# A GRU and two mixtures of experts on one core: weight loads in half-megabyte parts, recurrent weights in natural order, and a shorter set-up

## The chip, the cores and the metric

The kernel runs as one program on one core of a Trainium2 chip. The metric is the device time of one execution in microseconds (us), lower is better. It is written in Bass: each engine has its own instruction list, and every dependency between engines is a semaphore that the kernel sets and waits for by hand.

## The reference, cut to what matters

x is [4, 512, 512] (batch, time, features), D = 512. Three things are computed one after another:

```python
def cell(h, x):                       # scan over 512 time steps
    gi = x @ W_ih + b_ih              # does not depend on h
    gh = h @ W_hh + b_hh
    r = sigmoid(i_r + h_r); z = sigmoid(i_z + h_z)
    n = tanh(i_n + r * h_n)
    h_new = (1 - z) * n + z * h
x = x + ffn0(hs)     # x @ W.T + a mixture of 8 LoRA experts of rank 16, top 2
x = x + ffn1(interp(x, grid))   # linear interpolation along features, then per token
    # the top 2 of 8 experts: h = x @ w1[e].T + b1[e] (1024 columns), y = glu(h), y @ w2[e].T + b2[e]
```

All inputs are float32. The kernel splits an operand into a high and a low float16 part (scaled by 16 for activations, 64 for weights) and takes three products (high by high, low weight by high, high weight by low) in place of one float32 product.

## The kernel before, in words

**Order of the work.** The recurrence is a chain of 512 steps that cannot be shortened by other work, so everything else is hung between its steps by hand. The 512 steps fall into 4 groups of FT = 128. A step `gru(t)` is, on PE, 16 matmuls with the low recurrent weights on an early high part of h (L611), 16 with the high weights on both parts of h (L617), both for the gates r and z, then 4 bias matmuls (L623) and 32 for the gate n (L629). Each writes 32 PSUM partitions, so four run side by side. DVE then transposes (L1281, L1285), sums (L1283), scans (L1287, L1293) and splits the new h; ACT makes the sigmoid and the tanh (L978, the line of the helper `run`). POOL copies h to a history tile (`keep`, L1664).

**Group 0 (steps 0 to 127)** carries the prelude. The input gates `gi` of 64 time steps are one visit: 144 matmuls of 256 columns (L639, `gi_piece`). Visit 0 is made before step 0, visits 1 to 7 are spread over the steps in slots (`FIRST = 16` steps a visit to step 63, `LATER = 21` after it). The expert weights (16 halves of 1536 KB) are loaded, split by ACT and DVE, and stored to HBM; tables such as `MOE_STORE`, `MOE_LOAD`, `X_LOAD`, `GI_STORE` and `ZERO` name the step at which SP issues each transfer.

**Groups 1 to 3** run steps 128 to 511, and between them the feed-forward part of the block of 128 time steps that the group before has finished. After a head of 29 steps come NT = 15 tiles of 128 picked tokens, one expert each, 6 steps (u = 0 to 5) a tile (`slot`): u 0 to 2 the 26 up matmuls (24 of 128x512, L840, and two bias matmuls L836 with 2 rows), u 3 and 4 the 12 down matmuls (L860), u 3 and 5 transposes (L822, L846) and parts of the neighbours. A tail of 9 steps gathers the results and adds them.

**The last block** runs without any recurrence, its 15 tiles back to back. It has 4 weight buffers where the groups have 2: the tiles of `whh` and `gi` are free by then.

**Weights.** A tile needs 3072 KB: `load_up` (L494) issues 1536 KB (L500), 512 KB (L501) and 4 KB of biases (L502) one behind the other, and `load_down` (L504) 1024 KB (L509). For the tiles from the ninth on, the expert's number is read from a tile into a register of SP first (`value_load`, L491). SP issues all this in the order of its own list; what paces it are the waits for `up_mm`, `down_mm`, `d_out` and `xt_mm`. The input gates come back in one transfer of 1536 KB (L523).

**Recurrent weights.** They lie in `whh` in an order of their own: for each of the 4 strips of 32 columns the three gates one behind the other, so that the moving operand of a matmul is one run of 256 or 128 columns (L612, L630). The split at the start writes that order (`strips`): 12 activations of 128x512 and 48 DVE operations of 128x128 (L1646).

**The start.** SP loads the first third of `W_ih`, then x, six small arrays, the other two thirds, three constants and the three thirds of `W_hh` (L397 to L407), 1024 KB each third. PE waits for `x_split` and `wih_split`, makes visit 0, then a bias row through two matmuls of its own (L947), and waits for `whh_split` 3 before step 0 (L950). ACT makes `gates_now(0, 0)` (L1252) once all of this is out.

Of the kernel before, what the change touches and what calls it, by code (L numbers as in the profile page):

```python
# [24 lines left out]
UPW = K * 2 * D  # L25
PER = 5
# [37 lines left out]
def loads(f, j):  # L64

    if f < FB - 1:
# [5 lines left out]
VISITS = (0, 7, 6, 5, 1, 4, 3, 2)  # L72
KEPT = (0, 4, 7)
FIRST, LATER = 16, 21
# [29 lines left out]
X_LO = [s + q for s in (13, 21, 35, 56, 67, 91) for q in range(2)]  # L104
# [3 lines left out]
           for j, s in enumerate(at)}  # L108
# [11 lines left out]
X_LOAD = {2: 2, 16: 3, 30: 4, 38: 5, 59: 6, 69: 7}  # L120
L0_LOAD = {3: 0, 17: 1, 35: 2, 57: 3}
GRID_LOAD = {7: 1, 39: 2, 66: 3}
GI_STORE = {14: (1, 0), 19: (1, 1), 28: (2, 0), 32: (2, 1), 41: (3, 0), 49: (3, 1), 78: (5, 0), 86: (5, 1), 96: (6, 0),
            115: (6, 1)}
ZERO = {s: j for j, s in enumerate((5, 8, 11, 15, 18, 20, 21, 22, 25, 29, 31, 42, 45, 48, 51))}
ROW_STORE = {B2_AT + 3: 0, B1_AT + 5: 1}
PUT = {s for table in (MOE_STORE, MOE_LOAD, X_LOAD, L0_LOAD, GRID_LOAD, GI_STORE, ZERO, ROW_STORE) for s in table}
# [8 lines left out]
GIS = {v: pieces(G3, len(GI), n) for v, n in [(1, FIRST - 2)] + [(v, FIRST if v < 5 else LATER) for v in range(2, NB)]}  # L136
GIS[1] = [[], []] + GIS[1]

# [6 lines left out]
def visit(s):  # L145

    v, at, n = (1 + s // FIRST, s % FIRST, FIRST) if s < TB else (5 + (s - TB) // LATER, (s - TB) % LATER, LATER)
    return (v, at, n) if v < NB else (None, 0, 0)
# [12 lines left out]
def adaln_ffn_kernel(nc, x, h0, grid, w_ih, w_hh, b_ih, b_hh, w_base, lora_a, lora_b, w_router,  # L161
# [7 lines left out]
    with ctx:  # L169
# [41 lines left out]
        bias_w = sb("bias_w", [P, K], F32)  # L211
        bias_s = sb("bias_s", [P, 2, K], F16)
# [58 lines left out]
        b1s = upto[:, 0:E].rearrange("p e (g k) -> p e g k", g=2)  # L271
        spare_rows = hxs[:, FB % 2].rearrange("p a k b t -> p (a k b t)")
# [17 lines left out]
        bias_d = x1_f[:, 3 * D:4 * D].bitcast(F16).rearrange("p (w k n) -> p w k n", w=2, k=K)  # L290
        bias_at = gm[:, 1, 0, 0, 0:2 * P].rearrange("p (w n) -> p w n", w=2)
# [7 lines left out]
        def unit(i, n=1):  # L299
# [46 lines left out]
            const_in bias_in b2_in mix_zero l0_in x_in grid_in block_in row_stored zeroed  # L346
# [48 lines left out]
        def _(sp):  # L395
# [155 lines left out]
            for f in range(FB - 1):  # L551
# [4 lines left out]
                if f:  # L556
                    store_out(f - 1)
# [1248 lines left out]
```

## Time and profile before

| | |
|---|---|
| median of the 3 runs | 1904.66 us |
| all runs | 1902.78, 1904.66, 4286.78 us |
| the profiled execution's own time | 1901.47 us |
| its span in the trace | 1899.6 us |
| granted TensorE clock, mean | 0.999 |
| busy: PE, DVE, ACT, POOL | 91%, 69%, 41%, 16% |
| step 0 starts on PE | 36.01 us |
| steps 0 to 511 | 36 to 1699 us |
| last block | 1699 to 1899.6 us |

Times in the views are microseconds from the start of the span. PE is the matmul part of TensorE, PEld its weight loads, DVE VectorE, ACT ScalarE, POOL GpSimd, SP the engine that issues the transfers. "L611" is line 611 of the kernel. A busy PE is not PE at its peak: matmuls are pipelined, and one of 128x512 that is shown with 0.38 us starts some 0.22 us after its neighbour. An idle time ahead of an instruction is followed by what ended it; "issue" means that the engine waited for nothing that the profile shows.

### The profile page before, as it was taken

The numbers are of one execution on the slowest core, as the hardware profiler recorded it, in microseconds if no ns is written. First come the engines' busy times: TensorE is split into PE (matmuls) and PEld (weight loads), VectorE is DVE, ScalarE is ACT, GpSimd is POOL, SyncE is SP. The second block draws the span as 40 slices with busy tenths as digits, with TensorE's granted clock in tenths as the row PEclk, the third lists the DMA queues.
The fourth block names the chain that finished last, engine by engine and source line by source line (L and its number), as shares of the span: only waits on it lengthen the run. The fifth ranks groups of instructions, "written<-read, shape, count | busy, mean of one in ns | idle before, by whom it ended". The sixth has DMA issues, their size and how long they took to land.

```text
span 1899.6 us, 94495 instructions
## 1 busy us (share of the span) xinstructions
PE 1728.6 (91%) x40920; PEld 1153.3 (61%) x40920; DVE 1302.3 (69%) x5832; ACT 777.1 (41%) x2709; POOL 299.8 (16%) x601
## 2 busy tenths in 40 slices
PE   5888888878889999998999999988999999988998
PEld 4666676666556566656666566655666566654444
DVE  6788887877767676777766667777777666764323
ACT  5555566643334343332333343432334334323343
POOL 2222222221211111121211001121211001121001
PEclk9999999999999999999999999999999999999999
DMA  6445334345225465426134565426136445339993
GB/s 246 148 165 197 134 147 187 154 176 191 97 88 214 173 227 200 158 76 220 64 129 162 192 232 183 161 66 206 59 138 224 162 176 215 111 96 371 404 372 112
DMA packets 112945, 333.97 MB, mean 176 GB/s; under 512 B 41848, under 2 KB 42000, under 8 KB 100112
## 3 DMA queue, kind: packets, MB, share of 16 engines
q1 hardware_dynamic: 107408, 311.15, 45.0%
q0 software_dynamic: 5120, 16.78, 2.7%
q8 instruction: 320, 5.24, 1.1%
q14 instruction: 97, 0.79, 0.1%
HBM read 263.09 MB, written 64.78 MB: 173 GB/s over the span
## 4 chain that ended last, share of the span: by engine, by line
PE 70%; DVE 16%; ACT 6%; issue 5%; DMA 2%; DVEq 0%; SPq 0%; POOL 0%; ACTq 0%
PE bank L840 17%; PE bank_g L611 15%; PE bank_g L617 12%; PE bank L860 8%; PE bank_g L629 7%; DVE xt L1281 5%; DVE na L1287 3%; DVE pre L1283 3%; ACT rz L978 3%; DVE hs_early L1293 3%; ACT seq_h L978 3%; PE bank L654 2%; PE bank L836 2%; PE bank_l L846 2%; PE bank L822 2%
## 5 line engine op out<-in xcount | busy, mean ns | idle before, releaser
L1664 POOL COPY hxs<-hs 128x32 f16<-128x32 f16 x512 | 225.7, 441 | 1385.8 <-DVE hs L1301 1385.6
L978 ACT ACTIVATE rz<-pre 128x32 f32<-128x32 f32 x512 | 125.7, 245 | 750.9 <-DVE pre L1283 750.1
L611 PE MATMUL bank_g<-whh,hs_early 128*32 128x256 f16 x8192 | 319.0, 275 | 113.2 <-DVE hs_early L1293 110.3
L1281 DVE STREAM_TRANSPOSE xt<-bank_g 128x256 f32<-128x256 f32 x512 | 230.6, 450 | 226.6 <-PE bank_g L617 216.3
L611 PEld LDWEIGHTS bank_g<-whh,hs_early 128*32 128x32 f16 x8192 | 172.0, 96 | 298.7 <-DVE hs_early L1293 287.4
L629 PE MATMUL bank_g<-whh,hs 128*32 128x128 f16 x16384 | 323.3, 219 | 14.6 <-issue 14.4
L617 PE MATMUL bank_g<-whh,hs 128*32 128x256 f16 x8192 | 315.0, 273 | 4.3 <-issue 4.1
L840 PE MATMUL bank<-wm,wih 128*128 128x512 f16 x1272 | 308.6, 381 | 5.2 <-issue 3.0
L629 PEld LDWEIGHTS bank_g<-whh,hs 128*32 128x32 f16 x16384 | 257.4, 97 | 19.4 <-issue 18.5
L617 PEld LDWEIGHTS bank_g<-whh,hs 128*32 128x32 f16 x8192 | 206.4, 96 | 25.8 <-issue 5.7
L978 ACT ACTIVATE seq_h<-na 128x16 f32<-128x16 f32 x512 | 115.1, 225 | 215.9 <-DVE na L1287 215.9
L1293 DVE TENSOR_TENSOR_SCAN hs_early<-omz,seq_h 128x32 f16<-128x32 f32 x512 | 119.7, 234 | 104.9 <-ACT seq_h L978 104.7
L840 PEld LDWEIGHTS bank<-wm,wih 128*128 128x128 f16 x1272 | 110.0, 98 | 131.1 <-issue 15.2
L978 ACT ACTIVATE wih<-bank 128x512 f32<-128x512 f32 (+2 forms) x208 | 145.0, 701 | 90.5 <-PE bank L822 39.4
L1287 DVE TENSOR_TENSOR_SCAN na<-rz,xt_n 128x48 f32<-128x48 f32 x512 | 132.0, 258 | 72.9 <-ACT rz L978 3.9
L1285 DVE STREAM_TRANSPOSE xt_n<-bank_g 128x128 f32<-128x128 f32 x512 | 162.6, 318 | 14.6 <-PE bank_g L629 14.3
L639 PE MATMUL bank<-hxs,wih 128*128 128x256 f16 x1152 | 151.1, 278 | 16.1 <-DVE hxs L1306 13.0
L860 PE MATMUL bank<-wm,wih 128*128 128x512 f16 x636 | 154.0, 380 | 1.4 <-issue 1.4
L1283 DVE TENSOR_REDUCE pre<-xt 128x32 f32<-128x96 f32 x512 | 129.6, 253 | 17.6
L639 PEld LDWEIGHTS bank<-hxs,wih 128*128 128x128 f16 x1152 | 103.6, 99 | 41.7 <-DVE hxs L1306 13.0
L978 ACT ACTIVATE xt<-gi 128x32 f32<-128x32 f32 x512 | 123.7, 242 | 0.0
L1301 DVE TENSOR_TENSOR hs<-hh,hs_early 128x16 f16<-128x16 f32 x512 | 119.9, 234 | 0.0
(237 smaller groups left out, 2062.3 us busy)
## 6 DMA issues: line engine op xcount, KB each, us to landing
wm<-moe_split SPq DMA_DIRECT2D x53, 1536.0 KB
wm<-moe_split SPq DMA_DIRECT2D x53, 1024.0 KB, 6.4
wm<-moe_split SPq DMA_DIRECT2D x53, 512.0 KB
wm<-in_w_moe SPq DMA_DIRECT2D x16, 1536.0 KB, 6.8
moe_split<-wm SPq DMA_DIRECT2D x16, 1536.0 KB, 5.7
wih<-x_rows SPq DMA_DIRECT2D x58, 256.0 KB, 7.8
y_rows<-wih SPq DMA_DIRECT2D x58, 256.0 KB, 4.2
xr<-in_x SPq DMA_DIRECT2D x16, 512.0 KB, 6.7
```

Of the source, the lines that this page charges most:

```text
L611: mm(bank_g[0][32 * j:32 * j + 32, 0:2 * P], early_cols[:, 8 * B * k:8 * B * (k + 1)], whh[:, 1, k, at:at + 2 * P], start=(k == 0), stop=F ...
L617: i = mm(bank_g[0][32 * j:32 * j + 32, 0:2 * P], hs_cols[:, 8 * B * k:8 * B * (k + 1)], whh[:, 0, k, at:at + 2 * P], start=False, stop=(k ...
L629: i = mm(bank_g[1][32 * j:32 * j + 32, 0:P], hs_cols[:, 8 * B * k:8 * B * (k + 1)], whh[:, w, k, at:at + P], start=False, stop=(k == K - 1 ...
L639: i = mm(bank[m % len(bank)][:, 0:N], wih[:, w, k, m * P:(m + 1) * P], xs[v % 2][:, a, k], start=(j == 0), stop=(j == len(GI) - 1))
L840: mm(bk[:, :], xgt[:, a, k], weights(f, j)[:, at // HALF, w, up_at(at)], start=(c == 0), stop=False)
L860: i = mm(bank_down[:, :], yt[:, a, k], weights(f, j)[:, 1, w, up_at(UPW + k * D)], start=(n == 0), stop=(n == len(DOWN) - 1))
L978: return nc.scalar.activation(dst, src, func, **kw)
L1281: link(V.transpose(rows, bank_g[0][:, 0:2 * P].rearrange("p (m c) -> p m c", c=32)))
L1283: V.tensor_reduce(pre[:, :, :], terms, AX, ALU.add).then_inc(S["rz_pre"], 1)
L1287: V.tensor_tensor_scan(pairs["na"], pairs["r"], pairs["seq_n"], 0.0, ALU.mult, ALU.add).then_inc(S["n_pre"], 1)
L1293: V.tensor_tensor_scan(early_scan, pairs["omz"], pairs["seq_h"], 0.0, ALU.mult, ALU.add).then_inc(S["h_hi"], 1)
L1664: Q.tensor_copy(hxs[:, par, :, :, :, col].rearrange("p s k b -> p s (k b)"), hs_new).then_inc(S["h_kept"], 1)
```

## The change

- The start is reordered. x comes first, then `W_ih` in four parts (512, 512, 1024 and 1024 KB), h, the recurrent bias twice as a row, `W_hh` in three parts, and the small arrays and constants last. POOL makes the sum of the gate biases.
- Only the first 32 of the 64 time steps of the first visit are made ahead (visit 0, 144 matmuls of 128 columns); the other 32 are visit 1, in steps 0 to 7, 18 matmuls a step. The next four visits have 14 steps each (`WINDOW`) where they had 16.
- `whh` keeps its natural order. Its split is 3 activations and 3 DVE operations of 128x2048; the moving operand of a recurrent matmul is now 8 runs of 32 columns (r and z) or 4 runs (n and the bias), a run every 128 columns (`strip`).
- The bias row is built on POOL, ACT and DVE, without matmuls.
- A tile's weights come in 6 parts of 512 KB (`load_up` 4, `load_down` 2), each [128, 2, 1024] float16. In groups 1 to 3 SP waits for `h_ready` ahead of every step's transfers and issues one part a step (`load_head`, `load_slot`); the blocks of x and out and the gates come in parts of 512 KB too. In the prelude, the halves of 1536 KB are loaded and stored in two parts, in steps that follow each other. In the last block the parts are issued without such waits. `expert_of` is called for each part.
- The bias matmuls of the up product have 128 rows where they had 2; the other 126 rows are cleared once, by POOL, at step 120 and in group 3 behind step 19.
- Some steps of the tables move by a few.

```diff
-VISITS = (0, 7, 6, 5, 1, 4, 3, 2)
-KEPT = (0, 4, 7)
-FIRST, LATER = 16, 21
+VISITS = (0, 0, 7, 6, 5, 1, 4, 3, 2)
+WINDOW = {1: (0, 8), 2: (8, 14), 3: (22, 14), 4: (36, 14), 5: (50, 14), 6: (64, 21), 7: (85, 21), 8: (106, 21)}
...
-MOE_LOAD = {s + (3 if n < 13 else 2): n + 2 for s, n in MOE_STORE.items() if n + 2 < 2 * E}
+MOE_LOAD = {s + (2 if n in (6, 10, 11, 12, 13) else 3): n + 2 for s, n in MOE_STORE.items() if n + 2 < 2 * E}
+MOE_PUT = {s + part for table in (MOE_STORE, MOE_LOAD) for s in table for part in range(2)}
...
-        def strips(w, q, k):
-
-            by_strip = whh[:, w, k].rearrange("p (j g m c) -> p g m j c", j=K, g=3, c=32)
-            return by_strip[:, q]
+        def strip(v, j):
+
+            return v.rearrange("p (g j c) -> p j g c", j=K, c=32)[:, j]
...
         def _(sp):
+            sp.dma_start(xv, x[0]).then_inc(S["x_in"], 16)
+            for c in range(2):
+                sp.dma_start(wih_part(wm32[0], c), wih_part(w_ih, c)).then_inc(wih_in[c], 16)
+            for dst, src in ((bi[:, :], b_ih), (bh[:, :], b_hh)):
+                sp.dma_start(dst, src).then_inc(S["gate_bias_in"], 16)
+            for c in range(2, 4):
+                sp.dma_start(wih_part(wm32[0], c), wih_part(w_ih, c)).then_inc(wih_in[c], 16)
+            sp.dma_start(h_in, h0.rearrange("p k b -> p (k b)")).then_inc(S["h0_in"], 16)
+            sp.wait_ge(S["bias_zero"], 1)
+            for row in range(2):
+                sp.dma_start(bias_f[32 * row:32 * row + 1, :].rearrange("o (m p) -> o m p", m=K),
+                             b_hh[:, 2 * K:].rearrange("p (o m) -> o m p", o=1),
+                             allow_slow_non_contiguous=True).then_inc(S["bias_row_in"], 16)
             for q in range(3):
...
+            def load_half(n, part):
+                lo, hi = part * HALF // 2, (part + 1) * HALF // 2
+                sp.dma_start(wm32[0][:, n % 2 * HALF + lo:n % 2 * HALF + hi], w_moe[n, :, lo:hi]
+                             ).then_inc(stage_in[n % 2], 16)
...
+            def load_up(f, j, n):
+                if n == 0 and (f or j > 1):
                     sp.wait_ge(S["up_mm"], 2 * (f * NT + max(j + 1 - ring(f), 0)))
                 e = expert_of(f, j)
...
+                sp.dma_start(place_of(f, j, n), piece_of(e, n)).then_inc(up_in[j % ring(f)], 16)
+                if n == K - 1:
+                    if j in (0, 2):
+                        sp.wait_ge(S["rows_zero"], 1 if j % ring(f) < 2 else 2)
+                    sp.dma_start(ring_b[j % ring(f)][0:2], up_bias[e]).then_inc(up_in[j % ring(f)], 16)
...
+            def load_slot(f, j, u):
+
+                g = f + 1
+                if u == 0 and 1 <= j < NT - 1:
+                    load_up(f, j + 1, K - 1)
+                if u == 0 and j in (7, 9, 11) and g + 1 < FB:
+                    gi_load(2 * g + 2, 0, (j - 7) // 2)
+                if u in (1, 2) and j >= 2:
+                    load_down(f, j, u - 1)
+                if u == 1 and j >= 2:
+                    store_y(f, j - 2)
+                if u == 2 and j + 2 < NT:
+                    load_rows(f, j + 2)
+                if u >= 3 and j + 2 < NT:
+                    load_up(f, j + 2, u - 3)
...
             for f in range(FB - 1):
...
+                for s in range(20):
+                    sp.wait_ge(S["h_ready"], (f + 1) * FT + s + 1)
+                    load_head(f, s)
                 for j in range(NT):
...
+                    for u in range(SLOT):
+                        sp.wait_ge(S["h_ready"], (f + 1) * FT + HEAD + j * SLOT + u + 1)
+                        load_slot(f, j, u)
...
                     for j in range(K):
-                        at = j * 3 * P
-                        mm(bank_g[0][32 * j:32 * j + 32, 0:2 * P], early_cols[:, 8 * B * k:8 * B * (k + 1)],
-                           whh[:, 1, k, at:at + 2 * P], start=(k == 0), stop=False)
+                        mm(out_strip(0, j, 2 * P), early_cols[:, 8 * B * k:8 * B * (k + 1)],
+                           strip(whh[:, 1, k, 0:2 * D], j), start=(k == 0), stop=False)
...
                     if k is None:
-                        mm(bk[:, :], ones_as[0:2, :], ring_b[j % ring(f)][0:2, half * D:(half + 1) * D],
+                        mm(bk[:, :], ones_as[:, :], ring_b[j % ring(f)][:, half * D:(half + 1) * D],
                            start=False, stop=True).then_inc(S["up_mm"], 1)
...
+            x_hi(0)
+            wih_hi(0)
+            wih_hi(1)
+            wih_hi(2)
+            act.wait_ge(S["bi_ready"], 1)
+            gi_out(0, 0)
+            gi_out(0, 1)
+            wih_hi(3)
...
+            whh_hi(2)
+            for m in range(9, G3):
+                gi_out(0, m)
+            x_hi(2)
             act.wait_ge(S["gi_done"], G3)
             gates_now(0, 0)
...
-            for q in range(3):
-                for k in range(K):
-                    dve.wait_ge(S["whh_hi"], q * K + k + 1)
-                    for m in range(K):
-                        i = stt_(strips(1, q, k)[:, m], part_of(wm32[1], q)[:, k, m * P:(m + 1) * P].rearrange(
-                            "p (j c) -> p j c", c=32), WS, strips(0, q, k)[:, m], ALU.mult, ALU.subtract)
-                i.then_inc(S["whh_split"], 1)
+            whh_lo(0)
+            dve.wait_ge(S["bias_hi"], 1)
+            low = slice(32, 32 + 1)
+            stt_(bias_n[low], bias_f[low], WS, bias_n[low], ALU.mult, ALU.subtract).then_inc(S["bias_row"], 1)
+            whh_lo(1)
+            whh_lo(2)
             for s in range(FT):
...
+                if f == FB - 2:
+                    pool.wait_ge(S["l0_mm"], (f + 1) * K)
+                    Q.memset(spare_rows[:, 0:4 * D], 0.0).then_inc(S["rows_zero"], 1)
```

Here `wih_part` is `part_of` with the first gate cut in two, `out_strip` names the same PSUM region as before, `x_of(v)` is the number of the x load that visit v uses, and `piece_of` and `place_of` are part n of an expert's weights in HBM and in the buffer. `load_head` does for the first 20 steps of a group what `load_slot` does for the tiles: the block's x in steps 0 and 1, the last block's out in steps 2 and 3, the 12 parts of tiles 0 and 1 in steps 4 to 15, the gates in 16 to 18, the wait for `scattered` and the first rows in 19.

## Rows read from the trace of the kernel before

**Rows 1.** The profile's page: the chain that ended last, by engine

```profile
PE 70%; DVE 16%; ACT 6%; issue 5%; DMA 2%; DVEq 0%; SPq 0%; POOL 0%; ACTq 0%
```

**Rows 2.** Windows: length, busy PE, PEld, DVE, ACT, POOL, clock, DMA share, GB/s

```profile
447.00:865.00 418.00, 394.69 (x9838) 256.86 (x9836) 294.89 (x1400) 153.59 (x608) 60.57 (x144) 1.00 0.45 159
...
1780.00:1820.00 40.00, 40.00 (x232) 18.34 (x231) 13.51 (x21) 14.62 (x21) 0.00 (x0) 1.00 1.01 388
```

**Rows 3.** Timeline, steps 1 and 2: start, length, engine, line, tiles, count

```profile
42.27 0.62 PE L611 MATMUL bank_g<-whh,hs_early 128*32 128x256 f16 x16 [1.57 <-DVE hs_early L1293]
...
43.77 1.27 PE L639 MATMUL bank<-hxs,wih 128*128 128x256 f16 x10
...
45.41 0.62 PE L611 MATMUL bank_g<-whh,hs_early 128*32 128x256 f16 x16 [0.38 <-DVE hs_early L1293]
...
45.85 0.61 PE L617 MATMUL bank_g<-whh,hs 128*32 128x256 f16 x16
```

**Rows 4.** Waits of PE (total us, times, longest): issue, first and last of seven

```profile
PE bank_g L629 <- issue: 14.4, 21, 1.6
...
PE bank_g L623 <- issue: 1.0, 1, 1.0
```

**Rows 5.** Timeline of PE around one such wait

```profile
636.83 0.56 PE L629 MATMUL bank_g<-whh,hs 128*32 128x128 f16 x28
638.72 0.24 PE L629 MATMUL bank_g<-whh,hs 128*32 128x128 f16 x4 [1.33 <-issue]
```

**Rows 6.** Window ahead of it, columns as in rows 2

```profile
630.50:636.00 5.50, 5.50 (x132) 3.35 (x128) 4.46 (x21) 2.22 (x10) 0.33 (x1) 1.00 0.94 336
```

**Rows 7.** Timeline of SP's issues ahead of it

```profile
626.87 0.55 SPq L501 DMA_DIRECT2D wm<-moe_split  x1
...
632.73 0.55 SPq L509 DMA_DIRECT2D wm<-moe_split  x1
```

**Rows 8.** The profile's page: the queue of PE's instructions (packets, MB, share)

```profile
q8 instruction: 320, 5.24, 1.1%
```

**Rows 9.** Timeline of PE, slots u = 1 and 2 of a tile

```profile
604.24 0.62 PE L611 MATMUL bank_g<-whh,hs_early 128*32 128x256 f16 x16
...
605.73 1.47 PE L840 MATMUL bank<-wm,wih 128*128 128x512 f16 x6
607.13 0.39 PE L836 MATMUL bank<-brow,ones_as 2*128 2x512 f16 x1
607.44 0.62 PE L611 MATMUL bank_g<-whh,hs_early 128*32 128x256 f16 x16
```

**Rows 10.** Timeline of PE, last block, one tile to the next

```profile
1749.33 0.39 PE L836 MATMUL bank<-brow,ones_as 2*128 2x512 f16 x1
...
1758.85 0.39 PE L836 MATMUL bank<-hxs,ones_as 2*128 2x512 f16 x1
```

**Rows 11.** Timeline of the start

```profile
14.13 1.91 ACT L978 ACTIVATE wih<-wm 128x2048 f16<-128x2048 f32 x1 [5.03 <-DMA wm<-in_w_ih]
...
16.07 2.29 DVE L1623 SCALAR_TENSOR_TENSOR wih<-wm,wih 128x2048 f16<-128x2048 f32 x1 [3.17 <-ACT wih L978]
...
22.12 2.95 DVE L1635 TENSOR_SCALAR upto<-upto 128x32 f32<-128x32 f32 x1
...
26.17 9.79 DVE L1646 SCALAR_TENSOR_TENSOR whh<-wm,whh 128x128 f16<-128x128 f32 x48
...
36.01 0.62 PE L611 MATMUL bank_g<-whh,hs_early 128*32 128x256 f16 x16 [0.65 <-DVE whh L1646]
...
36.99 0.62 PE L629 MATMUL bank_g<-whh,hs 128*32 128x128 f16 x32
...
38.86 0.23 DVE L1293 TENSOR_TENSOR_SCAN hs_early<-omz,seq_h 128x32 f16<-128x32 f32 x1 [0.21 <-ACT seq_h L978]
```

**Rows 12.** Window over the first 21 us, columns as in rows 2

```profile
0.00:21.00 21.00, 6.76 (x48) 5.29 (x48) 8.32 (x7) 9.15 (x8) 3.89 (x14) 1.00 0.90 299
```

**Rows 13.** SP's register loads in the last block: ns min/median/max

```profile
L491 SPq TENSOR_LOAD <-eid x14: 273/430/445, 1781.3 to 1851.9; - x14
```

More of the change, by code:

```diff
@@ L25 @@
 UPW = K * 2 * D
+WIDTH = 1024
 PER = 5
@@ L103 @@
 GRID_HAT = {s + 3 + 4 * k: (b, k) for b, s in enumerate(GRID_START) for k in range(K)}
-X_LO = [s + q for s in (13, 21, 35, 56, 67, 91) for q in range(2)]
+X_LO = [s + q for s in (13, 31, 40, 56, 67, 91) for q in range(2)]
 L0_AT = (10, 24, 44, 65)
@@ L133, in pieces @@
     return [flat[s * len(flat) // slots:(s + 1) * len(flat) // slots] for s in range(slots)]
-GIS = {v: pieces(G3, len(GI), n) for v, n in [(1, FIRST - 2)] + [(v, FIRST if v < 5 else LATER) for v in range(2, NB)]}
-GIS[1] = [[], []] + GIS[1]
+GIS = {v: pieces(G3, len(GI), n) for v, (first, n) in WINDOW.items()}
 def ended(v, at):
@@ L145, in visit, with x_of @@
 def visit(s):
-    v, at, n = (1 + s // FIRST, s % FIRST, FIRST) if s < TB else (5 + (s - TB) // LATER, (s - TB) % LATER, LATER)
-    return (v, at, n) if v < NB else (None, 0, 0)
+    for v, (first, n) in WINDOW.items():
+        if first <= s < first + n:
+            return v, s - first, n
+    return None, 0, 0
+def x_of(v):
+    return max(v - 1, 0)
 def before(h, par):
@@ L366, in adaln_ffn_kernel @@
         gathered = [sem(f"gathered_{b}") for b in range(B)]
-        wih_in = [sem(f"wih_in_{gate}") for gate in "rzn"]
+        wih_in = [sem(f"wih_in_{part}") for part in ("r_a", "r_b", "z", "n")]
         whh_in = [sem(f"whh_in_{gate}") for gate in "rzn"]
@@ L438, in _ @@
             sp.dma_start(g_in, grid[0:1].to_broadcast([P, D])).then_inc(S["grid_in"], 16)
-            sp.wait_ge(S["wih_split"], 3)
-            load_half(0)
-            load_half(1)
+            sp.wait_ge(S["wih_split"], 4)
+            for n in range(2):
+                for part in range(2):
+                    load_half(n, part)
             sp.wait_ge(S["zero_set"], 1)
@@ L579, in _ @@
             sp.wait_ge(S["h_ready"], FB * FT + 1)
-            load_block(f)
-            store_out(f - 1)
+            for q in range(2):
+                load_block(f, q)
+            for q in range(2):
+                store_out(f - 1, q)
             for j in range(LAST_RING):
-                load_up(f, j)
-                load_down(f, j)
+                for n in range(K):
+                    load_up(f, j, n)
+                for n in range(2):
+                    load_down(f, j, n)
             sp.wait_ge(S["scattered"], FB * B * 2 * 16)
@@ L1358, in prelude @@
                 if s in (0, 1):
-                    x_lo(1, s)
+                    x_lo(2, s)
+                if s == 0:
+                    dve.wait_ge(S["bias_in"], 16 * 3)
+                    step(ts_(b1s[:, :, 1], b1s[:, :, 1], 1.0, None, ALU.add))
+                    step(ts_(bg[:, :], bg[:, :], PS, None, ALU.mult))
                 if s == B2_AT + 1:
@@ L1634, in _ @@
             step(V.memset(rz[:, 0:K * B, 1:GROUP - 1], 1.0))
-            step(ts_(b1s[:, :, 1], b1s[:, :, 1], 1.0, None, ALU.add))
-            step(ts_(bg[:, :], bg[:, :], PS, None, ALU.mult))
+            step(V.memset(ws_col[:, :], WS))
+            x_lo(0, 0)
+            x_lo(0, 1)
+            for c in range(4):
+                wih_lo(c)
+            dve.wait_ge(S["h0_in"], 16)
             step(ts_(hh[:, :, 1:2], h_in.unsqueeze(2), AS, None, ALU.mult))
```

324 lines of the change are left out of this document (156 added, 168 removed).

## The prediction

> **What bounds the kernel now.** I read the chain that ended last first [rows 1]: 70% of it is PE, 16% DVE, 6% ACT, and 5% is "issue", time in which an engine had work and nothing to wait for. By stage [rows 2], a group of 128 steps takes 418 us with the transfers at a share of 0.45, while the last block runs with them at 1.01. A step of the recurrence is fixed by its own chain: L611 starts at 42.27 and again at 45.41, 3.14 us later, and with ten matmuls of a visit in it PE still waits 0.38 us for h [rows 3]. 512 such steps are 1607 us. From 36 to 1699 us are 1663, so the steps lose some 56 us in all. Half of that can be named: in the view of waits PE stands at "issue" in seven groups of 36 waits, from 14.4 us (21 waits, up to 1.6) down to 1.0, which sum to 27.7 us [rows 4].
>
> One of them close up [rows 5]: L629 is cut after 28 of its 32 matmuls at 636.83, and the last 4 come at 638.72, with 1.33 us of nothing between. The transfer engines were at 0.94 in the 5.5 us before [rows 6], because SP had issued the 1536 KB of L500 and behind them the 512 KB of L501 at 626.87, and 1024 KB more at 632.73 [rows 7]. PE's own instructions come over the same 16 engines: 320 packets, 5.24 MB, so 16 KB a packet [rows 8], one every 5.9 us. My reading: a packet that is asked for while one large transfer fills the engines comes when that transfer is through, 3 to 4 us late, and PE's store of instructions covers less than that.
>
> **Parts of 512 KB, one a step.** At the 388 GB/s of a full queue [rows 2] 512 KB take 1.4 us, and with rows or y (256 KB) in the same step 2.1 us. Then the engines are free until the next step, 3.14 us after the last. A packet waits 2 us at most where it waited 4. The bytes stay the same: 3584 KB a tile over six steps is 195 GB/s, half of what the queue gives. Bounds: nothing gained, and all 27.7 us. I take 23: a few will be left in the prelude, where a part is 768 KB (2.1 us) and can meet a gate store of 768 KB or an x load, and where a gate part and a weight part fall in one step. SP has 1.3 us of work for a part with a register load (0.43 for the load [rows 13], 0.3 for the checks behind it, 0.55 for the transfer [rows 7]), of 3.14. The last up part goes out at u = 0 and is needed at u = 5, the down parts eight steps ahead of their use; 15 and 25 us are many times what the data take. The new waits on `h_ready` stand in SP's list only, and behind them are only the transfers of later steps; `store_y` and `load_rows` move by at most two steps within buffers that are two tiles deep. Nothing for them.
>
> The Trainium skill speaks against both halves of this. Its page "Runtime: NRT & Kernel Launch", section Instruction fetch mechanics, says that blocks of 16 KB are fetched ahead and that crossing a block is mostly hidden; by it the waits at issue have another cause and the sum loses its 23 us. The block size agrees with the trace; the rest I don't take, since the gap stands behind a stretch of full engines [rows 5, 6]. Its page "DMA: Bandwidth & Descriptors", section Bandwidth, advises transfers of 1 MiB and more for three quarters of the peak. In the groups half the peak is enough; in the last block it would matter (a rival below).
>
> **The bias matmuls of 128 rows.** In a row of 128x512 matmuls one starts every 0.217 us (six in 1.47, of which the last shows 0.385) [rows 9]. The sixth of these starts at 606.81 and L836 at 607.13, 0.31 later; L611 follows after 0.31 again. The next step's start is 3.20 us after the last where rows 3 have 3.14. So a change to 2 rows and back costs PE 0.1 us each way. With 128 rows the matmul itself costs the same, for its 512 columns set its time. In the groups two steps of a tile are long by 0.06 to 0.08: 90 x 0.07 = 6.3 us. In the last block PE alone sets the pace: a tile follows the last after 9.52 us [rows 10], with three such intervals in it (ahead of and behind the first bias matmul, ahead of the second): 15 x 3 x 0.1 = 4.5 us. Bounds: 0, and 10.8 + 15 x 0.1 = 12.3. I take 10.8. The clearing by POOL falls into its long waits for h.
>
> **The start.** Now the low part of `W_hh` ends last: DVE makes it from 26.17 on for 9.79 us, PE starts at 36.01, the step's first new h at 38.86, 1.87 after L629 [rows 11]. After the change it is one chain behind the transfers. 512 + 3072 + 3072 KB are 6.82 MB; 21 us brought 6.28 MB [rows 12], so the last third of `W_hh` lands at 22.5, and I add 1.5 for 1024 pieces of 4 bytes (no row shows such a load; bounds for it nothing, and the whole gain). Then 1.91 on ACT, 2.29 on DVE, 0.1, and 1.9 from the n matmuls to the new h [rows 11]: 30.2 against 38.86, 8.7 less. ACT has three `gi_out`, `x_hi(2)` and the gates to make in the same 4 us. PE's clock may be granted at half for a microsecond or two, since PE has less to do here; in the start before, it has gaps too. I take 8.5, bounds 0 and 10.3.
>
> What this moves into the steps: 18 matmuls of 128 columns in steps 0 to 7 are no more columns than 9 of 256, and ten of 256 fit with 0.38 us over [rows 3]; the windows of 14 steps hold 10 or 11, with 0.27 over. The 2.95 us of `b1s` [rows 11] move to step 0, where DVE has under 1 us free; it was beside POOL's clearing then and may well be shorter. Some table steps move. I put 0.5 us on all of it, bounds 0 and 4.
>
> **Natural order.** The moving operand is now in runs of 32 columns, 64 bytes. No row has a strided moving operand. A bound below zero I see no reason for: four matmuls side by side, 0.44 us for 16 [rows 3], are at 0.11 us for 256 columns, the pace of a lone one. Above: a break can hardly cost more than a new matmul does. Ten of 256 columns in 1.27 us are 0.111 each, 512 columns are 0.217, so 5 ns of 0.111 are the matmul's own. Four rounds in L611 and four in L617 of 7 breaks each are 56 breaks, 0.28 us a step, 143 us in all. I take 0, the value of contiguous rows. The skill's page "SBUF — State Buffer" counts in lines of 16 bytes, which runs of 64 bytes fill; by it the cost is none, and no run here shows it yet.
>
> **The sum.** 23 + 6.3 + 4.5 + 8.5 - 0.5 = 41.8 us. The profiled execution took 1901.5 (span 1899.6): 1859.7. The median of the runs is 3.2 above that execution: 1862.9, and I say 1862.
>
> **Rivals.**
> 1. *The stalls stay.* If the packets are late for another reason, or a part of 512 KB holds them up as well, 23 us are missing: 1885. For it: the queue is full for 1.4 to 2.1 us of each step now, so more packets meet a transfer than before. Against: every stall that I looked at ends behind a stretch at 0.9 or more that lasts longer than that. 0.25.
> 2. *The last block is bound by its transfers or by SP.* A tile takes 9.52 us [rows 10] and 3584 KB, 385 GB/s, where the queue gave 388 at a share of 1.01 [rows 2]. With 9.2 us a tile PE asks for 399, and all parts now have runs of 2 KB. SP needs, for each of the last 7 tiles, 6 x 1.3 + 0.5 + 0.6 + 0.5 = 9.4 us. Either way the 4.5 us are lost and perhaps as much again: 1872. Against it: tiles are loaded four ahead, 38 us, and 11 x 0.3 to 0.5 us are eaten from that. 0.14.
> 3. *Runs of 32 columns are read more slowly.* Place: L611 and L617 of each step, on the chain (DVE waits for the last of L617). Price: 0.28 us a step at 5 ns a break, 2006 us in all; from 1.5 ns a break on, 0.08 us a step, it takes back all that the rest gives, and the kernel is slower. Nothing in the trace speaks for it or against it. 0.06.
>
> **Chances.** My forecast 0.55, the rivals 0.25, 0.14 and 0.06. What a measurement of this kernel tells from no change is about 2%, 38 us: faster by it means below 1866.6. Of my own case four fifths lie below that (its own range is 1852 to 1872), of rival 2 a fifth, of rival 1 hardly any, and a larger gain at the start than I counted adds a little: 0.52. Slower by 2% is most of rival 3: 0.05. The range goes from 1848 (all stalls gone and 10 us at the start, 1853, with room for gains that I put at nothing) to 1888 (rival 1).
>
> **What would show it.** PE's waits at issue: from 27.7 us to about 5. The share of the transfers in a group stays near 0.45, without stretches of 5 us at 0.9. A step with a bias matmul as long as one without, and 9.2 us a tile in the last block. L611 and L617 still 0.44 us for 16; anything more there is rival 3, and it stands in every step. The first new h at 30 us. A step of 3.14 us outside the head and the tail. Wrong is the forecast if waits at issue stay above 15 us, if L617 grows, or if in the last block PE waits for weights.

## The result, and the profile after

The changed kernel took **1857.8 us** (median of 4 runs, 1855.86 to 1859.82), the kernel before 1906.34 us beside it (median of 4 runs, 1902.78 to 4286.78, the longest of which the ratio leaves out); the ratio is 0.975, 95% interval 0.9733 to 0.9768. The prediction said 1862, from 1848 to 1888. The profiled execution took 1857.5 us with a span of 1855.7, so 43.9 us of span are gone, where the sum had 41.8.

First the page's chain that ended last, by engine:

```profile
PE 68%; DVE 16%; ACT 7%; issue 4%; DMA 2%; SPq 1%; DVEq 0%; POOL 0%; ACTq 0%; POOLq 0%
```

"issue" is still 4%, some 74 us, so most of it stands in no wait of the next view. The waits of PE say more (line, what ended them, us in total, times, longest):

```profile
PE bank_g L691 <- issue: 4.2, 6, 1.0
PE bank L885 <- DMA wih<-x_rows: 2.5, 3, 1.0
...
PE bank L702 <- issue: 0.6, 2, 0.3
PE bank_l L999 <- issue: 0.5, 1, 0.5
```

The three groups at issue sum to 5.3 us in 9 waits; before they were 27.7 in 36 [rows 4]. Most of what went was in the tiles of groups 1 to 3: 19.3 us before, 1.8 now. A new wait stands among PE's, 2.5 us for rows in the last block.

Windows of group 1 and of 40 us of the last block, columns as in rows 2, and the queues (packets, MB, share):

```profile
439.00:845.00 406.00, 389.89 (x9827) 255.16 (x9820) 294.23 (x1397) 153.11 (x604) 60.15 (x144) 1.00 0.54 163
1780.00:1820.00 40.00, 37.35 (x224) 18.15 (x223) 8.30 (x12) 16.36 (x22) 0.00 (x0) 1.00 0.94 345
...
q1 hardware_dynamic: 171144, 311.17, 52.5%
...
q8 instruction: 321, 5.26, 1.2%
```

Group 1 takes 406 us where it took 418 [rows 2]. Its transfers move the same bytes, but their share is 0.54, not 0.45: the data are cut into more and smaller packets, and the engines are busy longer for the same bytes. In the last block the share and the rate fell, and PE has gaps (37.35 of 40 us busy).

Timeline of steps, of the bias matmuls in the last block, and of the first and the last new h:

```profile
54.88 0.62 PE L675 MATMUL bank_g<-whh,hs_early 128*32 128x256 f16 x16 [0.46 <-DVE hs_early L1372]
...
58.02 0.62 PE L675 MATMUL bank_g<-whh,hs_early 128*32 128x256 f16 x16 [0.38 <-DVE hs_early L1372]
...
58.46 0.61 PE L680 MATMUL bank_g<-whh,hs 128*32 128x256 f16 x16
...
1716.20 0.38 PE L899 MATMUL bank<-hxs,ones_as 128*128 128x512 f16 x1
...
1725.39 0.38 PE L899 MATMUL bank<-hxs,ones_as 128*128 128x512 f16 x1
...
32.31 0.23 DVE L1372 TENSOR_TENSOR_SCAN hs_early<-omz,seq_h 128x32 f16<-128x32 f32 x1 [0.21 <-ACT seq_h L1041]
...
1657.16 0.23 DVE L1372 TENSOR_TENSOR_SCAN hs_early<-omz,seq_h 128x32 f16<-128x32 f32 x1 [0.21 <-ACT seq_h L1041]
```

A step is 3.14 us, and L680 starts 0.44 behind L675, as before [rows 3]. A tile of the last block follows after 9.19 us, not 9.52 [rows 10]. The first new h comes 6.55 us earlier [rows 11]. From the first to the last it is 1624.85 us; before it was 1660.11 (38.86 to 1698.97). The rest of the span is 198.5, before 200.6. So 6.55 us come from the start, 35.3 from the steps, 2.1 from the last block.

The start on SP and ACT, from the timeline:

```profile
5.84 7.42 SPq L422 DMA_DIRECT2D x<-in_b_hh  x2
...
13.31 2.57 SPq L426 DMA_DIRECT2D wm<-in_w_hh  x3
...
19.92 1.91 ACT L1041 ACTIVATE whh<-wm 128x2048 f16<-128x2048 f32 x1 [3.73 <-DMA wm<-in_w_hh]
```

SP needs 7.42 us to issue the two bias rows, of 2 KB each, and `W_hh` stands behind them. PE's clock is at the lower of its two levels in this stretch (clock, DMA share and GB/s are the last three):

```profile
22.23 2.55 PE L702 MATMUL bank<-hxs,wih 128*128 128x128 f16 x24 [4.04 <-ACT gi L1041]
...
30.60 0.24 PE L687 MATMUL bank_g<-bias_n,bias_to 128*32 128x128 f16 x4 [0.72 <-DVE whh L1709]
...
23.00:29.00 6.00, 5.03 (x53) 4.45 (x55) 4.97 (x4) 5.37 (x8) 0.99 (x2) 0.50 0.89 318
```

It fell at about 22.5 us, when PE had just stood 4.04 us for ACT, and rose at about 29.3. In the kernel before it was at half from about 22.6 to 26.0, where PE had stood 2.98 us. PE's last wait ahead of the first new h is for DVE's low part of `W_hh`, so little of the start hangs on the clock: in `bias_2_rows` below, which starts in the same way and had the full clock throughout, the first new h came at 31.57, 0.7 us earlier.

SP in the last block:

```profile
1779.45 4.69 SPq L538 DMA_DIRECT2D wm<-moe_split  x4
...
1785.67 1.89 SPq L548 DMA_DIRECT2D gi<-moe_split  x2
...
1789.44 4.58 SPq L538 DMA_DIRECT2D wm<-moe_split  x4
...
L521 SPq TENSOR_LOAD <-eid x168: 262/273/977, 652.4 to 1811.2; - x168
```

The four transfers of L538 are a tile's up parts, the two of L548 its down parts. One round of SP for a tile lasts 9.99 us (1779.45 to 1789.44), more than the 9.19 that PE wants.

### The profile page after: what moved, and what is told of

It reads as the page before. It is cut to its first block, busy times and chain, and to the rows that moved or that the text cites. A ratio compares the mean times of both kernels' runs of the same rounds, so it can differ in the third digit from the quotient of the medians.

```text
span 1855.7 us, 95597 instructions
## 1 busy us (share of the span) xinstructions
PE 1712.6 (92%) x41062; PEld 1158.1 (62%) x41062; DVE 1297.6 (70%) x5787; ACT 779.7 (42%) x2713; POOL 299.4 (16%) x599
## 3 DMA queue, kind: packets, MB, share of 16 engines
q1 hardware_dynamic: 171144, 311.17, 52.5%
## 4 chain that ended last, share of the span: by engine, by line
PE 68%; DVE 16%; ACT 7%; issue 4%; DMA 2%; SPq 1%; DVEq 0%; POOL 0%; ACTq 0%; POOLq 0%
PE bank L903 16%; PE bank_g L675 15%; PE bank_g L680 12%; PE bank L923 8%; PE bank_g L691 7%; DVE xt L1360 5%; DVE na L1366 3%; DVE pre L1362 3%; ACT rz L1041 3%; ACT seq_h L1041 3%; DVE hs_early L1372 3%; PE bank L717 2%; PE bank L899 2%; PE bank L885 2%; PE bank_l L909 1%
## 5 line engine op out<-in xcount | busy, mean ns | idle before, releaser
L675 PE MATMUL bank_g<-whh,hs_early 128*32 128x256 f16 x8192 | 318.0, 275 | 105.3 <-DVE hs_early L1372 104.5
L675 PEld LDWEIGHTS bank_g<-whh,hs_early 128*32 128x32 f16 x8192 | 171.4, 96 | 300.8 <-DVE hs_early L1372 295.6
L691 PE MATMUL bank_g<-whh,hs 128*32 128x128 f16 x16384 | 319.1, 219 | 4.2 <-issue 4.2
L680 PE MATMUL bank_g<-whh,hs 128*32 128x256 f16 x8192 | 312.6, 273 | 0.1
L691 PEld LDWEIGHTS bank_g<-whh,hs 128*32 128x32 f16 x16384 | 255.4, 97 | 6.7 <-issue 5.5
L680 PEld LDWEIGHTS bank_g<-whh,hs 128*32 128x32 f16 x8192 | 203.2, 96 | 22.5 <-DVE hs L1380 3.4
L903 PEld LDWEIGHTS bank<-wm,wih 128*128 128x128 f16 x1272 | 114.5, 98 | 123.4 <-ACT wih L1041 2.5
L702 PE MATMUL bank<-hxs,wih 128*128 128x256 f16 (+1 forms) x1296 | 154.4, 269 | 15.2 <-DVE wih L1703 9.5
L1362 DVE TENSOR_REDUCE pre<-xt 128x32 f32<-128x96 f32 x512 | 129.7, 253 | 17.8 <-ACT xt_n L1041 0.2
L702 PEld LDWEIGHTS bank<-hxs,wih 128*128 128x128 f16 x1296 | 109.5, 101 | 38.6 <-issue 13.4
```

The costliest lines, as they stand in the source:

```text
L675: mm(out_strip(0, j, 2 * P), early_cols[:, 8 * B * k:8 * B * (k + 1)], strip(whh[:, 1, k, 0:2 * D], j), start=(k == 0), stop=False)
L680: i = mm(out_strip(0, j, 2 * P), hs_cols[:, 8 * B * k:8 * B * (k + 1)], strip(whh[:, 0, k, 0:2 * D], j), start=False, stop=(k == K - 1))
L691: i = mm(out_strip(1, j, P), hs_cols[:, 8 * B * k:8 * B * (k + 1)], strip(whh[:, w, k, 2 * D:], j), start=False, stop=(k == K - 1 and w == 1))
L702: i = mm(bank[m % len(bank)][:, 0:B * n].rearrange("p (b t) -> p b t", b=B), wih[:, w, k, m * P:(m + 1) * P], xs[x_of(v) % 2][:, a, k].rea ...
L903: mm(bk[:, :], xgt[:, a, k], weights(f, j)[:, at // HALF, w, up_at(at)], start=(c == 0), stop=False)
L1362: V.tensor_reduce(pre[:, :, :], terms, AX, ALU.add).then_inc(S["rz_pre"], 1)
```

## Experiments

Two theories stand against each other for the largest term: what holds PE's instructions up is the bunching of the weight transfers (mine), or something else that changed with them. Then come the bias matmuls, the operand's order, and the two places in which the profile after shows SP as the late one. "First to last h" is the difference of the two starts of the scan that writes `hs_early`.

**1. Large transfers again** (`large_parts`).

```diff
-                sp.dma_start(place_of(f, j, n), piece_of(e, n)).then_inc(up_in[j % ring(f)], 16)
...
+                if n:
+                    return
...
+                sp.dma_start(w[:, 0], experts[e, :, 0]).then_inc(up_in[j % ring(f)], 16)
+                sp.dma_start(w[:, 1, :, 0:UPW - HALF], experts[e, :, 1, :, 0:UPW - HALF]).then_inc(up_in[j % ring(f)], 16)
...
```

> The changed kernel with the old transfer sizes (1536 + 512 KB for an up product, 1024 KB for a down product), each set issued in the step in which its first part went out; prelude, gates, blocks, bias matmuls and start stay new. If the size and bunching of the weight transfers caused PE's waits at issue: they go back from 5.3 us in 9 waits to about 25 us in 30, all in groups 1 to 3, and the groups are 22 us longer. In the last block SP has fewer transfers and register loads to issue: a tile follows the last after 9.2 us throughout, and the 2.5 us that PE waited there for rows are gone, so the whole stands at 1857.8 + 22 - 2.5 = 1877 us. If the stalls had another cause: waits at issue stay near 5 us and the whole is 1855 us.

Measured: 1883.07 us (ratio to the kernel before 0.9893, 0.9876 to 0.9909). PE's waits at issue, first two and last of nine groups:

```profile
PE bank_g L697 <- issue: 11.2, 16, 1.5
...
PE bank L891 <- issue: 2.7, 3, 1.4
...
PE bank_g L693 <- issue: 0.3, 1, 0.3
```

They sum to 24.4 us in 34 waits. First to last h: 1649.2 us, 24.4 more. From the last h to the end: 195.4 us, 3.1 less, and no wait for rows. Both halves came as expected. The time is 6 us over the expected one: 2.4 because I had set 22 us for 24.4, the rest within the spread of the runs (1878.5 to 1884.24; the profiled one is the lowest).

**2. The same parts, but in one step** (`parts_at_once`).

```diff
-                if u >= 3 and j + 2 < NT:
-                    load_up(f, j + 2, u - 3)
+                if u == 3 and j + 2 < NT:
+                    for n in range(K):
+                        load_up(f, j + 2, n)
```

and both down parts at u = 1, in the heads of the groups likewise.

> The changed kernel with the same parts of 512 KB, but in groups 1 to 3 all four up parts in one step and both down parts in one step. If what matters is how long the engines are filled without a pause: the same waits at issue as with the large transfers, about 25 us, 1857.8 + 22 = 1880 us (SP needs some 1.2 us a part, in which the queue can drain 512 KB at 388 GB/s in 1.4 us: no pause forms). If what matters is the size of the single transfer: waits at issue stay near 5 us and the time is 1858 us. In between, some 8 to 15 us, if the pauses between issues let some packets through. The last block is as it was.

Measured: 1877.63 us (ratio 0.9859, 0.9842 to 0.9875). First to last h 1649.7 us, 24.8 more than with parts spread out, and waits at issue of 22.6 us; the largest group:

```profile
PE bank_g L693 <- issue: 14.1, 16, 2.8
```

So the size of a single transfer is not what matters. Parts of 512 KB behind each other do what one of 1536 KB does; the pauses between them are worth the 24 us.

**3. Weight transfers cut to 64 columns in the groups** (`thin_parts`, on the kernel of run 1; apart from the first load of each buffer, the experts' weights in groups 1 to 3 are mostly those of an earlier tile).

```diff
+                thin = (f or j > 1) and f < FB - 1
+                a, b = (64, 64) if thin else (HALF, UPW - HALF)
...
-                sp.dma_start(w[:, 0], experts[e, :, 0]).then_inc(up_in[j % ring(f)], 16)
+                sp.dma_start(w[:, 0, :, 0:a], experts[e, :, 0, :, 0:a]).then_inc(up_in[j % ring(f)], 16)
...
```

> The kernel with the large transfers, but in groups 1 to 3 each weight transfer brings 64 columns of its 1024 to 3072 (16 KB in place of 512 to 1536; the first load of each of the two buffers and all loads of the last block stay whole), so most of the matmuls of the experts there use weights of an earlier tile. Every instruction, wait and count stays. If the weight transfers are what holds PE's instructions up: the 24.4 us at issue go down to under 3, the groups take 1623 us or less (1624.9 in the changed kernel, 1649.2 with large transfers), and the whole is 1883 - 26 = 1857 us, or 1855 with the stalls that the changed kernel still has. If the waits at issue have another cause, such as the order of PE's own instructions: 1880 us.

Measured: 1852.03 us (ratio 0.9716, 0.9694 to 0.9738), first to last h 1622.4. A thin transfer brings 32 KB in the trace, not the 16 of the expectation. All waits at issue:

```profile
PE bank_g L700 <- issue: 2.4, 3, 1.0
...
PE bank L711 <- issue: 0.6, 2, 0.4
...
PE bank_g L684 <- issue: 0.6, 1, 0.6
```

3.6 us, a little over the 3 I gave, with every instruction in its place. The stalls come from the weights' transfers. It also bounds what is left: the changed kernel's steps are within 2.5 us of a kernel that hardly loads weights.

What it is that comes late the traces of these kernels show too, for they hold the start and the length of every packet of PE's instruction queue. From 45 us on, the kernel before has 32 waits at issue of 0.25 us and more, run 1 has 28, run 2 has 25 and the changed kernel 8. Each of these 93 ends 1.2 to 1.6 us after such a packet has landed. Two windows of the kernel before, ahead of the wait of rows 5, which ends at 638.72: all queues that were at work from 630.95 to 636.3, and the queue of instructions from 636.3 to 636.4 (packets, MB, share):

```profile
q1 hardware_dynamic: 614, 1.77, 92.3%
...
q8 instruction: 1, 0.02, 68.2%
```

In the 5.35 us of the first window no packet of the instruction queue starts. The next starts at 636.33, lands at 637.42, and PE goes on 1.30 us later. A packet takes about 1 us (median 0.99, ahead of a wait 0.95), so it isn't slow itself; its start is late, 7.0 us after the last packet's in the median, where all packets of that kernel are 5.3 us apart.

**4. Bias matmuls of 2 rows** (`bias_2_rows`).

```diff
-                        mm(bk[:, :], ones_as[:, :], ring_b[j % ring(f)][:, half * D:(half + 1) * D],
+                        mm(bk[:, :], ones_as[0:2, :], ring_b[j % ring(f)][0:2, half * D:(half + 1) * D],
```

> The changed kernel with bias matmuls of 2 rows again. Theory of the prediction: a change to 2 rows and back costs PE 0.1 us each way: two of six steps of a tile are longer by 0.06 to 0.08 us, 6.3 us in the groups; in the last block 0.3 us a tile while PE sets the pace (the first 8 tiles, 2.4 us) and nothing more where SP does. 1857.8 + 8.7 = 1866.5 us. Rival: the groups save more than the sum of the prediction (35.3 us measured against 28.7), and this could be the part that gives more: then the groups are 13 us longer and the whole 1873 us. Rival: steps with bias matmuls were long because of large transfers only: no change, 1858 us.

Measured: 1866.55 us (ratio 0.9804, 0.9788 to 0.9821). First to last h 1630.2 us, 5.3 more (31.57 to 1661.75); from there to the end 200.8, 2.3 more. Two rows of the last block:

```profile
1721.62 0.38 PE L899 MATMUL bank<-hxs,ones_as 2*128 2x512 f16 x1
...
1731.14 0.39 PE L899 MATMUL bank<-hxs,ones_as 2*128 2x512 f16 x1
```

9.52 us a tile again. The first theory holds in both places, and the change of row count is not where the additional microseconds are. (The total fits its expectation better than the parts do: of the 8.7 us between the medians, the profiled executions show 6.9.)

**5. One run per moving operand** (`one_run`; the recurrence computes something else, as the expectation says).

```diff
-            return v.rearrange("p (g j c) -> p j g c", j=K, c=32)[:, j]
+            return v.rearrange("p (j g c) -> p j g c", j=K, c=32)[:, j]
```

> The changed kernel with the moving operands of the recurrent matmuls and of the bias of the n gate as one run of 256 or 128 columns in place of 8 or 4 runs of 32 (the columns that a strip reads are then others, so the recurrence computes something else; all counts and shapes stay). If runs of 32 columns cost nothing: 1857.8 us, 16 matmuls of 256 columns start over 0.44 us as before. If a break costs 0.5 ns: 56 breaks a step on the chain, 14 us less. The routing of tokens to experts changes with the values, but not the number of tiles.

Measured: 1857.94 us (ratio 0.9756, 0.974 to 0.9773), against 1857.8. Eight runs of 64 bytes are read as fast as one of 512. This settles the third rival, as the trace after does from the other side (0.44 us for 16, as before).

**6. One register load for several parts** (`one_register`).

```diff
                 if j + LAST_RING < NT:
+                    e = expert_of(f, j + LAST_RING)
                     for n in range(K):
-                        load_up(f, j + LAST_RING, n)
+                        load_up(f, j + LAST_RING, n, e)
```

and the two down parts likewise.

> The changed kernel; in the last block the expert's number is read into a register once for the four up parts of a tile and once for the two down parts, in place of once for each part. If SP's time to issue set the pace of the last tiles (10.0 to 11 us a tile, with 0.43 us for a register load and 0.3 us of checks behind it, six times): four of six go, 2.9 us a tile, SP needs some 7.5 us a tile, all tiles follow at 9.2 us and PE's waits for rows (2.5 us in all) are gone: 1855.3 us. Rival: the transfers themselves bind there (3584 KB in 9.2 us are 399 GB/s): PE then waits for weights or rows as before, 1857.8 us.

Measured: 1854.94 us (ratio 0.974, 0.9722 to 0.9758), expected 1855.3. SP's timeline, a round later in the block:

```profile
1784.10 2.73 SPq L538 DMA_DIRECT2D wm<-moe_split  x4
...
1788.39 1.28 SPq L548 DMA_DIRECT2D wm<-moe_split  x2
```

2.73 us for four parts where it took 4.69. PE has no wait for rows left, and from the last h to the end it is 195.4 us, as with the large transfers. So it was SP's time to issue, not the transfers.

**7. `W_hh` ahead of a single bias row** (`start_early`).

```diff
-            for row in range(2):
...
             for q in range(3):
+                if q == 2:
+                    sp.dma_start(bias_f[0:1, :].rearrange("o (m p) -> o m p", m=K),
...
                 sp.dma_start(part_of(wm32[1], q), part_of(w_hh, q)).then_inc(whh_in[q], 16)
```

> The changed kernel; at the start two thirds of the recurrent weights are issued ahead of the bias row, and the row is loaded once, not twice (the low part is made from the same partition). SP spent 7.42 us on the two rows, and the first third of the recurrent weights was issued only at 13.31 us. Now it goes out at 5.8 us, the last third some 6 us later than the first. If SP's time on the rows held the start up: the first third is there when ACT is free for it (16.2 us instead of 19.9), the first new h comes at 28.5 to 29.5 us instead of 32.31, and the whole is 1854.5 us. If the transfers' rate sets it (6.8 MB at 300 GB/s, the last third at 22.5 us): the first new h at 29.5 to 30.2. If neither: no change, 1857.8 us.

Measured: 1857.35 us (ratio 0.9748, 0.973 to 0.9766): nothing. SP's timeline tells why:

```profile
8.09 1.78 SPq L423 DMA_DIRECT2D x<-in_b_hh  x1
...
9.92 8.40 SPq L426 DMA_DIRECT2D wm<-in_w_hh  x1
```

The row itself now takes 1.78 us, but the transfer behind it stays at SP for 8.40. The first new h came at 31.42 us. (Other kernels with the start as changed have it between 31.18 and 33.57, so this is no gain.) Some 0.5 us of that is the clock: from 27 to 33 us it was granted at 0.50, and the 32 matmuls ahead of the h took longer than in the changed kernel, where they took 0.63:

```profile
29.25 0.30 PE L687 MATMUL bank_g<-bias_n,bias_to 128*32 128x128 f16 x4 [4.47 <-DVE whh L1709]
29.31 1.09 PE L691 MATMUL bank_g<-whh,hs 128*32 128x128 f16 x32
```

Both edits 6 and 7 in one kernel:

> Both edits of the other two runs of this set. If they act at different places and each does what it should: 3.3 + 2.5 us less, 1852 us. If only one does: 1854.5 or 1855.3 us. In either case faster than both kernels.

Measured: 1852.93 us (ratio 0.9725, 0.9707 to 0.9742), 0.9 over the expectation. Run 7 by itself shows no gain, and the first new h came at 31.24 here, so I read the 2 us below run 6 as the spread of the runs (here 1851.28 to 1853.2, there 1854.24 to 1856.71), though the two ranges don't meet; the profiled executions are 1.0 us apart, in the steps.

**8. The bias row laid out in memory** (`row_laid_out`). The array's 512 numbers lie 12 numbers apart in `b_hh`; here a row of its own holds them.

```diff
...
-                             b_hh[:, 2 * K:].rearrange("p (o m) -> o m p", o=1),
-                             allow_slow_non_contiguous=True).then_inc(S["bias_row_in"], 16)
+                sp.dma_start(bias_f[32 * row:32 * row + 1, :], b_row).then_inc(S["bias_row_in"], 16)
```

> The changed kernel, but the bias row comes from an array of its own that holds its 512 numbers one behind the other (an array more at launch, laid out like the others there), so that each of the two loads is one piece of 2 KB and not 512 of 4 bytes. Loading the row once and behind two thirds of the recurrent weights did not help: then the load of the row took SP 1.78 us, and the last third, which stood behind it, 8.40 us, to 18.32. Theory: the 512 pieces hold up the issue of what comes behind them; the bytes do not. Then the two loads take SP about 1 us, all of the recurrent weights are issued by 10 us, the last third lands at 22 to 22.5 us, and the first new h comes 1.9 + 2.3 + 2.1 us later, at 28.5 to 29 us in place of 32.31: 1854.3 us. Rival: SP's issue is held by the bytes that are under way (3 MB and more): the last third is issued at 16 us or later again, and the first new h stays at 31 us: 1857 us.

Measured: 1854.4 us (ratio 0.973, 0.9711 to 0.9749), expected 1854.3. Timeline and, last, a window of 3 us:

```profile
5.36 0.62 SPq L422 DMA_DIRECT2D x<-in_b_row  x2
...
6.02 3.86 SPq L424 DMA_DIRECT2D wm<-in_w_hh  x3
...
22.47 1.91 ACT L1039 ACTIVATE whh<-wm 128x2048 f16<-128x2048 f32 x1 [0.99 <-DMA wm<-in_w_hh]
...
28.57 0.23 DVE L1370 TENSOR_TENSOR_SCAN hs_early<-omz,seq_h 128x32 f16<-128x32 f32 x1 [0.21 <-ACT seq_h L1039]
...
12.00:15.00 3.00, 2.86 (x29) 2.60 (x28) 2.29 (x1) 2.71 (x4) 0.00 (x0) 1.00 1.06 386
```

and the same window of the changed kernel:

```profile
12.00:15.00 3.00, 2.97 (x28) 2.70 (x26) 2.24 (x1) 2.47 (x4) 0.00 (x0) 1.00 0.33 42
```

There the queue had run dry (42 GB/s) while SP was at the rows. Now it stays full, and the first new h comes at 28.57, 10.3 us earlier than in the kernel before. The Trainium skill, page "DMA: Bandwidth & Descriptors", section Rules for kernel authors, says that a non-contiguous last dimension becomes one descriptor per element; the measurements agree: 2 x 512 elements took 7.42 us to issue, two whole rows 0.62. With the one register load as well:

> The row laid out, and in the last block one register load for the four up parts and one for the two down parts. If the row's layout is worth 3.5 us: 1854.9 - 3.5 = 1851.4 us. If it is worth nothing: 1854.9 us, as with the one register load alone.

Measured: 1852.72 us (ratio 0.9717, 0.9698 to 0.9736), with `both` the best of the kernels that compute what they should, 5 us below the changed kernel. It is 1.3 over the expectation: the first new h came at 29.39 here, and the steps took 1628.0 us.

**9. The heads of the groups** (`all_at_once`, `all_at_once_2`). What runs 1 and 4 leave open of the steps' 35.3 us.

```diff
+                if s == 0:
+                    for q in range(3):
+                        gi_load(2 * g + 1, 1, q)
...
-                if 16 <= s < 19:
-                    gi_load(2 * g + 1, 1, s - 16)
```

and the blocks, the stores of out and the other half of the gates likewise, on the kernel of run 1.

> The kernel with the large weight transfers, and beside them the gates, the blocks of x and the stores of out of a group issued all in one step again (the first of the group; the second half of the gates at tile 6), as in the kernel before. Groups 1 to 3 took 1251.9 us in the kernel before, 1218.6 in the changed one and 1242.5 with the large weight transfers; the bias matmuls account for 5.4 of the 33.3. If the heads of the groups make up what is left, 3.5 to 4 us: the groups take 1246 us and the whole 1887 us. If nothing comes of it: 1242.5 us and 1883 us, and the rest of 4 us lies elsewhere (the gathers at the end of a group).

> The same kernel as the run before this one. There the kernel before took 1946.33 us, 2% more than in all other sets, and this one 1933.55 with 42.4 us of waits at issue, so neither can be set against the other runs. If the kernel before stands at 1905 again: groups 1 to 3 take 1246 us and the whole 1887 us if the heads of the groups make up the 4 us that are left; 1242.5 and 1883 us if not.

Measured: 1933.55 us beside 1946.33 for the kernel before (ratio 0.9936, 0.9907 to 0.9965), and 1934.1 beside 1947.6 (0.9938, 0.9921 to 0.9954). In both sets the kernel before was 2% slower than elsewhere; the second set ran on the chip of `thin_parts` and `row_laid_out`, where it took 1906.31, so it isn't the chip. What slowed them isn't known, but the traces say where. By the starts of the new h, in us over groups 1 to 3 (a group has 29 steps of head, 90 of tiles, 9 of tail):

| | head | tiles | tail |
|---|---|---|---|
| before | 283.9 | 879.5 | 91.7 |
| changed | 280.0 | 851.9 | 90.0 |
| `large_parts` | 282.9 | 873.5 | 89.3 |
| `all_at_once` | 315.9 | 873.3 | 106.5 |
| `all_at_once_2` | 313.6 | 872.1 | 106.0 |

PE's waits at issue summed to 42.5 and 38.0 us, up to 3.4 us long, but in the tiles to 18.1 and 17.4, as in `large_parts` (17.8). There every one of 0.25 us and more ends 1.2 to 1.6 us after a packet of instructions; in the heads and tails 5 of 28 and 4 of 23 do. The additional waits are of another kind. The clock was lower as well: 0.990 in the mean, against 0.998 in `large_parts` (the kernel before: 0.989 to 0.995 in these sets, 0.996 to 1.0 in the others), with stretches at 0.50 behind long stops of PE (848.0 to 851.5 and 875.4 to 878.8 in the first; the second stretch follows a wait of 3.43 us). Group 0 took 406.2 and 407.0 us as ever. Whether the edit did any of this can't be told, since the kernel before was 41 us slower beside it: inconclusive.

## Why the prediction was right, step by step

| term | said | measured |
|---|---|---|
| stalls at issue | 23 | 22.4 by the waits (27.7 to 5.3); 24.4 and 24.8 us of steps by undoing it |
| bias, groups | 6.3 | 5.3 |
| bias, last block | 4.5 | 2.3; 2.1 for the block as a whole |
| start | 8.5 | 6.55 |
| moved things | -0.5 | group 0 is 2.0 shorter, not longer |
| groups 1 to 3, beyond the above | 0 | some 4 |
| sum | 41.8 | 43.9 |

- **Stalls.** The mechanism held as far as it was tested, and so did the size. The rival that they stay is refuted, and so is the sharper form of it, that a part of 512 KB does harm: it does only with others close behind. My picture had a flaw in it: the share of the transfers did not stay at 0.45 but rose to 0.54, with fewer stalls. The share is not what matters. The Trainium skill's rule that block crossings are mostly hidden ("Runtime: NRT & Kernel Launch", Instruction fetch mechanics) describes `thin_parts`, with 3.6 us left of 24.4; with bunched transfers the measurement differs from it and decides. That PE waits for its instructions, and that their packets start late behind bunches, the traces show (run 3). That a packet stands behind a large transfer until that is through was only argued: nothing here shows what holds its start up.
- **Bias matmuls.** 0.1 us a change held: with 2 rows the tiles of groups 1 to 3 took 857.5 us, with 128 rows 851.9, 5.6 less. In the last block the 4.5 us were there for PE (9.19 a tile), but from the ninth tile on SP needed 10 us a tile. That is the half of rival 2 that named SP, at 9.4 us; I had given the rival 0.14, and it took 3.1 us (198.5 to 195.4 with `one_register`), not 9, since the other tiles kept their gain. Its other half, the transfers, was wrong: with `one_register` PE waits for no rows and no weights at the same bytes. With it the block is 5.2 us shorter than before, close to the 4.5.
- **The start.** The step that failed: "I add 1.5 for 1024 pieces of 4 bytes", a term for which the prediction had no row. They cost SP 7.42 us, the queue ran empty behind them, and the first new h came at 32.31 in place of 30.2. Laid out, the start is worth 10.3 us, my upper bound.
- **Natural order.** Nothing, as said, by two ways.
- **What the sum lacked.** Of the steps' 35.3 us, run 1 gives 24.4 and run 4 gives 5.3. Group 0 has 2.0, of which 0.5 are in run 1's figure. Some 4 us are left in groups 1 to 3, which I had not costed; by the table of run 9, set against `large_parts`, 2.4 are in the tails and 1.0 in the heads. Their cause is open. So the total came within 2 us in part by luck, through errors that cancel: the start and the last block gave 4.3 less than said, the steps some 6 more.

## What to carry to other kernels

Where PE stands at "issue" behind a stretch of full transfer engines, and goes on soon after a packet of its instructions has landed, spread the transfers over the time they have, rather than shrink them: pauses between them were worth 24 us here, smaller pieces in one bunch nothing. Cutting a transfer costs the issuing engine: count its time for each piece with its register loads, and share one load among the pieces. And before a load is put ahead of others on a queue, look at how many separate pieces it has, not at its bytes: 4 KB in pieces of 4 bytes held 3 MB up.

## What the runs showed that I had not expected

- A load of 512 pieces of 4 bytes took SP 1.78 us to issue where it stood behind two thirds of `W_hh`, and then the next transfer, of 1024 KB, took 8.40; two such loads in a row took 7.42, and the transfers behind them 2.57 for three. The cost can show at the instruction behind.
- The same bytes in 1.6 times as many packets (171,144 to 107,408) raise the engines' share from 45.0% to 52.5% of the span, and cost the steps at most the 2.5 us that separate them from `thin_parts`.
- In the last two sets the kernel before took 41 us more than in all others. `all_at_once` was some 50 us over `large_parts` there, all of it in the heads and tails of the groups (422.4 and 419.6 us, against 372.2), none in the tiles, where most of the weights are loaded.
- Every one of 93 waits at issue in four kernels ends 1.2 to 1.6 us after a packet of PE's instructions has landed, so what such a wait is can be read from the queue of instructions.
